# Self-attention: first pass on a three-bank ring, some key pairs as rectified differences

## The reference

```python
qkv = h @ w_qkv + b_qkv
q, k, v = jnp.split(qkv, 3, axis=-1)
q = q.reshape(B, S, H, DK)
k = k.reshape(B, S, H, DK)
v = v.reshape(B, S, H, DK)
scores = jnp.einsum('bqhd,bkhd->bhqk', q, k) / np.sqrt(DK)
attn = jax.nn.softmax(scores, axis=-1)
o = jnp.einsum('bhqk,bkhd->bqhd', attn, v).reshape(B, S, D)
x = x + o @ w_o + b_o
```

## Time and profile before

| what | value |
|---|---|
| median of 3 runs | 2763.42 us (2761.18 to 2769.22) |
| profiled execution's own time | 2774.48 us |
| span of the profile | 2772.7 us |
| TensorE (matmul) busy | 2119.2 us, 76% |
| VectorE busy | 1248.5 us, 45% |
| ScalarE busy | 828.2 us, 30% |
| projection of queries, keys and values | about 538 to 598 us of the span |
| attention steps | about 606 to 1098 us of the span |

### The profile page before, as it was taken

How to read it: one execution, slowest core, us unless ns; L and a number is a source line. 1 busy time by engine, 2 the same in 40 slices (tenths; PEclk the granted TensorE clock), 3 DMA queues, 4 the chain that set the end, 5 groups by cost and what they waited for, 6 DMA issues and landing times. The chain is left out here.

```text
span 2772.7 us, 39418 instructions
## 1 busy us (share of the span) xinstructions
PE 2119.2 (76%) x11925; PEld 1548.1 (56%) x11929; DVE 1248.5 (45%) x2841; ACT 828.2 (30%) x1718; POOL 443.2 (16%) x363
## 2 busy tenths in 40 slices
PE   6689979368899898255999634899998981993398
PEld 5477746122222222144999533788888871683297
DVE  6856621868777773342333343222222222673221
ACT  2404421113555556001333210233333330341021
POOL 0100000010000000033222103334524530000322
PEclk9899989677999999557999865999999996995699
DMA  3012110130101100712222253222222212007111
GB/s 129 1 43 74 46 33 4 37 102 13 36 24 32 28 25 7 244 50 75 33 33 33 53 194 107 54 43 48 58 39 47 48 31 57 1 1 274 55 30 27
DMA packets 128820, 157.19 MB, mean 57 GB/s; under 512 B 24266, under 2 KB 108499, under 8 KB 128693
## 3 DMA queue, kind: packets, MB, share of 16 engines
q1 hardware_dynamic: 100661, 123.14, 14.3%
q0 software_dynamic: 28032, 32.60, 6.7%
HBM read 110.32 MB, written 57.24 MB: 60 GB/s over the span
## 5 line engine op out<-in xcount | busy, mean ns | idle before, releaser
L1454 PE MATMUL banks<-m_rowsT,x_normT 128*128 128x128 f32 x4032 | 487.0, 280 | 46.1 <-DVE m_rowsT L1516 22.9
L1454 PEld LDWEIGHTS banks<-m_rowsT,x_normT 128*128 128x128 f32 x4032 | 473.3, 195 | 76.8 <-issue 65.2
L1464 PE MATMUL banks<-e_w,m_hT 128*128 x2016 | 456.7, 379 | 3.6 <-ACT m_y L1549 2.6
L1464 PEld LDWEIGHTS banks<-e_w,m_hT 128*128 128x128 f32 x2016 | 373.1, 190 | 50.8 <-issue 5.4
L1539 ACT ACTIVATE m_hT<-banks,m_bias 128x128 f32<-128x128 f32 x848 | 241.1, 370 | 402.5 <-PE banks L1454 384.5
L1839 DVE TENSOR_REDUCE sh_mhalf<-banks 128x1 f32<-128x512 f32 x512 | 318.9, 684 | 76.1 <-PE banks L1742 71.4
L1817 ACT ACTIVATE sh_pT<-banks 128x1024 f32<-128x1024 f32 x256 | 249.5, 1021 | 210.5 <-PE banks L1795 210.5
L1411 POOL DMA_INDIRECT scratch_acc<-m_y,m_ids x106 | 175.8, 1659 | 538.0 <-ACT m_y L1549 487.2
L1520 DVE COPY m_ids<-m_rows 128x1 int32<-128x1 int32 x126 | 19.4, 154 | 509.7 <-POOLq L1417 410.5
L1742 PE MATMUL banks<-sh_ks,sh_qs 96*128 96x512 bf16 x512 | 196.1, 416 | 53.8 <-DVE sh_mhalf L1839 33.4
L1501 DVE TENSOR_SCALAR x_normT<-e_w 128x2048 f32 x129 | 159.7, 1238 | 137.6 <-PEq L1470 81.9
(11 more groups left out here) (317 smaller groups left out, 2485.5 us busy)
## 6 DMA issues: line engine op xcount, KB each, us to landing
e_w<-L_W SPq DMA_DIRECT2D x32, 1024.0 KB, 12.2
m_rows<-scratch_rows SPq DMA_DIRECT2D x126, 132.5 KB, 2.1
e_w<-L1f_W SPq DMA_DIRECT2D x16, 1024.0 KB, 12.1
a_bt<-bias SPq DMA_DIRECT2D x16, 616.0 KB, 4.1
scratch_parts<-sp_part SPq DMA_DIRECT2D x48, 128.0 KB, 1.9
sh_qs<-scratch_parts SPq DMA_DIRECT2D x96, 64.0 KB, 2.6
sh_ks<-scratch_parts SPq DMA_DIRECT2D x96, 64.0 KB, 2.7
scratch_acc<-x_resid SPq DMA_DIRECT2D x2, 2048.0 KB
```

The lines of the kernel that those rows point to most:

```text
L1454: mm = pe.matmul(ps[:, H_BANK + f // 4, f % 4 * P:(f % 4 + 1) * P], w1_tile[:, u, k, f * P:(f + 1) * P], rowsT[:, u, k, :], start=(k == 0) ...
L1464: mm = pe.matmul(ps[:, Y_BANK, 0:D], hT[:, u, f, :], w2_sb[:, bass.ds(e, 1), f, :], start=(f == 0), stop=(f == FB - 1))
```

## The change

In the **projection** ScalarE writes the high part straight from the bank (`high`), VectorE the rest (`rest`), ScalarE the middle (`middle`), VectorE the low (`low`). The orders are written with one chunk of lead: high(n), then middle(n-1); rest(n), then low(n-1). For keys ScalarE also writes the full values (`keys`), and VectorE takes the difference of keys 0 to 511 and keys 512 to 1023 (`step`), which goes through the same split and to DRAM (`store_steps`).

In the **first pass** a pair can be *rising*: its first product is with the key differences (`kd`), ScalarE takes Relu of it, and VectorE adds the second product and takes the row maximum in one operation, since max(a, b) = b + relu(a - b). All pairs of steps 0 and 1 are rising, and pairs 1, 4, 7, 10 and 13 of each later step. The banks are a ring of three (0, 1, 7), shared with the two turns, and of seven in the opening; ahead of step 0 TensorE waits for all of the opening's maxima. The two halves' maxima are joined by one operation and turned once; the split into parts is made after the turn by four linked operations on 16x128. Loads of differences come on SyncE's queue (18 transfers a step instead of 12); the queries of step 0 come on ScalarE's.

```diff
+RISING_PAIRS = (1, 4, 7, 10, 13)
...
+            r32, k32, d32 = sb2("r32", [P, 2, CH]), sb2("k32", [P, 2, CH]), sb2("d32", [P, 2, CH])
...
+            part_d = [sb2(f"part_d{i}", [P, 2, CH], BF16) for i in range(PARTS)]
...
+
+                def store_steps(m):
+                    j, b = 2 + m // 2, m % 2
+                    sp.wait_ge(d_split, m + 1)
+                    for i in range(PARTS):
+                        sp.dma_start(parts_d[i, (j % 2) * P:(j % 2 + 1) * P, b * CH:(b + 1) * CH], part_d[i][:, m % 2, :]).then_inc(d_stored[m % 2], 16)
+
                 for n in range(NQ):
                     j, c = n // NCH, n % NCH
                     sp.wait_ge(split, n + 1)
                     for i in range(PARTS):
                         sp.dma_start(parts[j // 2, i, (j % 2) * P:(j % 2 + 1) * P, c * CH:(c + 1) * CH], part[i][:, n % 2, :]).then_inc(stored[n % 2], 16)
+                    if n >= K0 + 3 and n % 2:
+                        store_steps((n - K0 - 3) // 2)
+                store_steps(3)
...
                     if n >= 4:
-                        pe.wait_ge(q_sb, n - 3)
+                        pe.wait_ge(rest_done, n - 3)
+                    if n >= K0 + 4:
...
                 w.wait(act)
-                for n in range(NQ):
-                    j = n // NCH
+
+                def high(n):
+                    j, u = n // NCH, n % 2
                     act.wait_ge(mm_done, n + 1)
                     if n >= 2:
-                        act.wait_ge(split, n - 1)
-                    act.activation(q32[:, n % 2, :], ps[:, n % 4, :], ACT.Identity, bias=bqk[:, j:j + 1]).then_inc(q_sb, 1)
+                        act.wait_ge(stored[u], 48 * (n // 2))
+                    act.activation(part[0][:, u, :], ps[:, n % 4, :], ACT.Identity, bias=bqk[:, j:j + 1]).then_inc(high_done, 1)
+
+                def keys(n):
+                    if n >= K0 + 2:
+                        act.wait_ge(d_done, (n - K0) // 2)
+                    act.activation(k32[:, n % 2, :], ps[:, n % 4, :], ACT.Identity, bias=bqk[:, n // NCH:n // NCH + 1]).then_inc(k_sb, 1)
+
+                def middle(n):
+                    act.wait_ge(rest_done, n + 1)
+                    act.copy(part[1][:, n % 2, :], r32[:, n % 2, :]).then_inc(middle_done, 1)
+
+                def step_high(m):
+                    act.wait_ge(d_done, m + 1)
+                    if m >= 2:
+                        act.wait_ge(d_stored[m % 2], 48)
+                    act.copy(part_d[0][:, m % 2, :], d32[:, m % 2, :]).then_inc(d_high, 1)
+
+                def step_middle(m):
+                    act.wait_ge(d_rest, m + 1)
+                    act.copy(part_d[1][:, m % 2, :], d32[:, m % 2, :]).then_inc(d_middle, 1)
+
+                for n in range(NQ):
+                    high(n)
+                    if n >= K0:
+                        keys(n)
+                    if n:
+                        middle(n - 1)
+                    if n >= K0 + 2 and n % 2 == 0:
+                        step_high((n - K0 - 2) // 2)
+                    if n >= K0 + 3 and n % 2:
+                        step_middle((n - K0 - 3) // 2)
+                middle(NQ - 1)
+                step_high(3)
+                step_middle(3)
...
+
+                def rest(n):
+                    j, u = n // NCH, n % 2
+                    dve.wait_ge(high_done, n + 1)
+                    if n >= K0:
+                        dve.wait_ge(k_sb, n - K0 + 1)
+                    if n >= 2:
+                        dve.wait_ge(split, n - 1)
+                    dve.scalar_tensor_tensor(r32[:, u, :], ps[:, n % 4, :], bqk[:, j:j + 1], part[0][:, u, :],
+                                             ALU.add, ALU.subtract).then_inc(rest_done, 1)
+
+                def low(n):
                     u = n % 2
-                    dve.wait_ge(q_sb, n + 1)
+                    dve.wait_ge(middle_done, n + 1)
                     if n >= 2:
                         dve.wait_ge(stored[u], 48 * (n // 2))
-                    link(dve.tensor_copy(part[0][:, u, :], q32[:, u, :]))
-                    link(dve.tensor_tensor(r32[:, u, :], q32[:, u, :], part[0][:, u, :], ALU.subtract))
-                    link(dve.tensor_copy(part[1][:, u, :], r32[:, u, :]))
                     dve.tensor_tensor(part[2][:, u, :], r32[:, u, :], part[1][:, u, :], ALU.subtract).then_inc(split, 1)
+
+                def step(m):
+                    dve.wait_ge(k_sb, 2 * m + 2)
+                    if m >= 2:
+                        dve.wait_ge(d_split, m - 1)
+                    dve.tensor_tensor(d32[:, m % 2, :], k32[:, 0, :], k32[:, 1, :], ALU.subtract).then_inc(d_done, 1)
+
+                def step_rest(m):
+                    dve.wait_ge(d_high, m + 1)
+                    dve.tensor_tensor(d32[:, m % 2, :], d32[:, m % 2, :], part_d[0][:, m % 2, :], ALU.subtract).then_inc(d_rest, 1)
+
+                def step_low(m):
+                    dve.wait_ge(d_middle, m + 1)
+                    if m >= 2:
+                        dve.wait_ge(d_stored[m % 2], 48)
+                    dve.tensor_tensor(part_d[2][:, m % 2, :], d32[:, m % 2, :], part_d[1][:, m % 2, :], ALU.subtract).then_inc(d_split, 1)
+
                 w.wait(dve)
+                for n in range(NQ):
+                    rest(n)
+                    if n:
+                        low(n - 1)
+                    if n >= K0 + 3 and n % 2:
+                        step_low((n - K0 - 3) // 2)
+                    if n >= K0 + 2 and n % 2 == 0:
+                        step_rest((n - K0 - 2) // 2)
+                    if n > K0 and n % 2:
+                        step((n - K0) // 2)
+                low(NQ - 1)
+                step_rest(3)
+                step_low(3)
                 for t in range(NT):
                     dve.wait_ge(v_mm, t + 1)
                     dve.tensor_tensor(vh[:, t, :, 0:DK], ps[:, 4 + t % 4, 0:D].rearrange("p (h d) -> p h d", d=DK),
...
-            A_BANK, B_BANK, O_BANK, T_BANK = 0, 2, 6, 7
+            B_BANK, O_BANK = 2, 6
+            OPENING, STEADY = (0, 1, 7, 2, 3, 4, 5), (0, 1, 7)
...
+            RISING = tuple(RISING_PAIRS if s >= 2 else range(2 * KT) for s in range(NP))
...
+            opening = [("a", 0, c) for c in range(NA)] + [("a", 1, c) for c in range(4)] + [("m", 0, 0)] + [("a", 1, c) for c in range(4, NA)]
+            steady = []
+            for s in range(NP):
+                for k in range(KT):
+                    steady += [("a", s + 2, 4 * k + c) for c in range(4) if s + 2 < NP]
+                    steady += [("m", s + 1, 0)] if k == 1 and s + 1 < NP else []
+                    steady += [("o", s - 1, 0)] if k == 2 and s else []
+            steady.append(("o", NP - 1, 0))
+            bank, user_before, last_user = {}, {}, {}
+            for i, use in enumerate(opening + steady):
+                bank[use] = OPENING[i % len(OPENING)] if i < len(opening) else STEADY[(i - len(opening)) % len(STEADY)]
+                user_before[use] = last_user.get(bank[use])
+                last_user[bank[use]] = use
+
+            def bank_free(pe, use):
+
+                old = user_before[use]
+                if old is None:
+                    return
+                kind, s, c = old
+                if kind == "m":
+                    pe.wait_ge(mT_sb, s + 1)
+                elif kind == "o":
+                    pe.wait_ge(on_done, s + 1)
+                elif c % 2 == 0 and c // 2 in RISING[s]:
+                    pe.wait_ge(a_rise, rise_count[s * NA + c + 1])
+                else:
+                    pe.wait_ge(a_max, max_count[s * NA + c + 1])
...
+                    steps = lambda i: parts_d[i, hp * 2 * DK:(hp + 1) * 2 * DK, b * CH:(b + 1) * CH].rearrange("(h p) n -> p h n", p=DK)
                     for j, (i, k) in enumerate(PROD):
-                        sp.dma_start(qs[u][j * DK:(j + 1) * DK, :, :], rows(0, i)).then_inc(stack_in[u], 16)
+                        sp.dma_start(kd[u][j * DK:(j + 1) * DK, :, :], steps(k)).then_inc(stack_in[u], 16)
+                        if s:
+                            sp.dma_start(qs[u][j * DK:(j + 1) * DK, :, :], rows(0, i)).then_inc(stack_in[u], 16)
                         sp.dma_start(ks[u][j * DK:(j + 1) * DK, :, :], rows(1, k)).then_inc(stack_in[u], 16)
...
+                bank_free(pe, ("a", s, c))
+                keys = kd[u][:, h, :] if half == 0 and c // 2 in RISING[s] else ks[u][0:SR, h, half * CH:(half + 1) * CH]
+                pe.matmul(ps[:, bank["a", s, c], :], qs[u][0:SR, h, t * P:(t + 1) * P], keys, start=True, stop=True).then_inc(a_mm, 1)
...
@@ -1748,26 +1875,25 @@
...
+                    bank_free(pe, ("m", s, 0))
+                    pe.transpose(ps[0:2 * KT, bank["m", s, 0], 0:P], m32[:], core.ident[:]).then_inc(mT_mm, 1)
...
+                    bank_free(pe, ("o", s, 0))
...
+                for c in range(4):
...
+                pe.wait_ge(a_rise, rise_count[2 * NA])
+                pe.wait_ge(a_max, max_count[2 * NA])
...
```

(42 more changed lines are left out.)

79 lines of the change are left out of this document (34 added, 45 removed).

## The result

| | median | runs | ratio to before, 95% interval |
|---|---|---|---|
| before | 2763.49 us | 2761.18 to 2769.22 | |
| changed | 2698.31 us | 2697.05 to 2704.05 | 0.9765 [0.9745, 0.9786] |

The change takes 65.2 us off. The prediction was 2725, range 2702 to 2756: the direction is right, the size is not, and the time lies 3.7 us under the range. A second measurement of the same kernel (experiment 1) gave 2703.97, inside the range.

The account below looks back on a forecast made before the run. The prediction took a latency bound, bank ring, reduction, bank ring, with no engine full. Terms: opening -18.5, step 0 -6.2, steps 1 to 13 -53, last two -0.2, projection +40, sum -38 us: 2725 us, range 2702 to 2756.

Parts of the forecast that it names:

- The bank ring bounds the steady step: Steady attention steps: the two-bank ring costs 0.67 us a block; three banks make a block 2.92 us, 3.5 less over six.
- new wait of score product 3: Blocks k = 0, 1 of a step: score product 3 waits 0.7 us for exponential 1, queued behind pair 1's Relu.
- The projection serialises on stores: Projection: the look-ahead order with two buffers puts one full store round trip into each chunk, +40 us.
- Rival 2: Projection: it does not serialise, because an order was misread, and keeps its pace; 2685 us, chance 0.07.
- rival 3: Steady steps: each Relu brings two table loads, as Relu and Exp are in different sets; 2825 us, chance 0.04.
- Step 0: First attention step after the opening: 26 us instead of 32.16 with TensorE kept busy, 6.2 us less.
- SyncE's queue hidden: Loads of differences: 18 x 0.467 = 8.4 us per step against 24.6, and the opening's 48 transfers, cost no time.
- The sum-and-max: Custom VectorE operation of the rising pairs: 0.75 us, 0.80 per pair with a wait in it.
- Rival 1: Opening and steps: sum-and-max at half rate, 1.29 us pitch; 33 us more, 2758 us, chance 0.13.
- The opening: First passes ahead of step 0: 32 pairs on seven banks at 0.80 us each, 18.5 us less.
- The steady step: Steps 1 to 13 of attention: 24.6 us instead of 28.71, 4.1 less each, 53 us less together.
- the difference is taken from either: Whole program: the same -38 us applied to the median (2725 us) or to the profiled execution (2736 us).

Follow-up runs that it names:

- experiment 1: The kernel before and the changed kernel each measured again with no edit: 2759.06 us (one run) and 2703.97 us (ratio 0.9781).
- Experiment 6: Changed kernel's later steps: two banks without rising pairs 2772.09 us, with five 2773.64; three banks without 2717.69, with five 2703.97.
- norise: Changed kernel with no rising pairs from step 2 on, three-bank ring and opening kept: 2717.69 us, ratio 0.9822 to the kernel before.
- experiments 3 to 5: Changed kernel with four buffers for the parts (2663.51 us), with the older chunk first on two buffers (2676.55), and with both (2660.19).
- before: The kernel before the change, in its first measurement and profile: median 2763.49 us.
- null_before: The kernel before, measured and profiled once more with no edit: 2759.06 us (one run).
- projonly: The changed kernel's projection in front of the attention of the kernel before: 2795.17 us, ratio 1.0107 to the kernel before.
- after: The changed kernel in its first measurement and profile: 2698.31 us, ratio 0.9765 to the kernel before.
- after_again: The changed kernel measured and profiled once more with no edit: 2703.97 us, ratio 0.9781 to the kernel before.

## Why the prediction came out as it did

**Right.**
- *The bank ring bounds the steady step.* Experiment 6 shows it by itself: 28.90 to 24.71. Blocks were forecast at 2.92, and those of k = 3 to 6 are 2.82 to 2.95 (k = 2 with the turns is 3.42, before 3.99; k = 7 with the step's last weighted sums 3.77, before 4.37); in the pair of blocks k = 0, 1 the forecast was 5.46 with a new wait of score product 3 for the exponential behind the Relu. It is 5.36 (814.23 to 819.59), and the wait is there, 0.43 us instead of 0.7:

```profile
817.52 0.60 PE L1921 MATMUL banks<-sh_qs,sh_ks 99*128 99x512 bf16 x2 [0.43 <-ACT sh_pT L1962]
```

  Without rising pairs (`norise`) that pair of blocks takes 5.42: the wait behind the Relu stands where a wait for a bank would stand.

- *The projection serialises on stores.* The walk put high(2) 6.7 us after the first chunk (measured 543.10 - 536.41 = 6.69), query chunks at 5.02 (4.97), key chunks at 5.62 (5.70 on average), the values 38.3 us later plus 1.4 for trips longer than the usual one (measured 38.5 in all, and 1.1 more in the values themselves). The 1.4 was not well founded: seven trips with one of 4.5 us have a mean of 3.2, not 3.05, and the earlier trace rows show only two of the seven. In the new trace one key chunk of seven took 0.5 us more than the others. Rival 2 (2685, no serialising) is refuted by the 43.7 us of waits, and experiments 3 to 5 turn the mechanism off in two ways. The Trainium skill ("DMA: Bandwidth & Descriptors", Anatomy of one DMA) gives its figures for a transfer that GpSimd issues, and by them a transfer would be 2.3 us, an estimate. These stores are issued by SyncE, which the prediction passed over; the row after is 1.9 again, and the chain by the row was the better one.
- *Relu brings no table load in the steps* (rival 3, 2825). ScalarE loads a table once in the attention stage, at its first exponential:

```profile
664.80 1.21 ACT L1950 ACTIVATE sh_rise<-banks 128x512 f32<-128x512 f32 x2
666.03 1.28 ACT L1962 ACT_TABLE_LOAD   x1
```

  That agrees with the Trainium skill ("ScalarE: Activation LUTs", Table sets), which lists relu in every set.
- *Step 0* at -6.2 (-6.3), and SyncE's queue hidden. That the number of step 0 fits this well is luck: in the repeat it is -7.6, with the clock's change at another place.

**Mis-sized.**
- *The sum-and-max.* I took 0.75, and 0.80 with waits, from the nearest three-operand row, though the range's lower end, a reduction's pitch of 0.60, was the truth: 0.61. The row that was nearer in shape (a 512-element read from PSUM with an accumulated result) was the reduction itself. Rival 1 (half rate, 2758) is refuted: one operand in PSUM and one in SBUF, both fp32, run at the full pitch, as the Trainium skill's sentence taken at its word allowed ("Vector Engine (DVE) Microarchitecture Reference", Points that are easy to get wrong).
- *The opening*: TensorE's pace at the lower clock counted for six pairs only, the sum-and-max was shorter, and the sum had a slip of 0.2 (its terms give 634.6, not 634.8). Six distances between pairs were about 0.85, most of the later ones 0.61, so that from the first sum-and-max to the first score product 22.6 us passed, not 27.3; the first one came 1.3 later than forecast, since the keys' stack landed later than I had it. VectorE's last sum-and-max starts at 666.69, the join of the maxima at 667.41, and the first score product 0.06 later: the new wait ahead of step 0 decides as the prediction said. -22.0 instead of -18.5.
- *The steady step*: 24.15 instead of 24.6. The six blocks gave 3.65 us, where 3.5 less 0.2 for the turn was forecast: the turn's bank held by the maxima costs about 0.1 and not 0.2 (the product behind the turn starts 0.54 after its score product, elsewhere 0.44). The pair k = 0, 1 gave 0.91 instead of 0.8. 13 x 0.46 = 6 us.

**The step that failed** is the last line of the sum: "the difference is taken from either", that is, from the median or from the profiled execution. With the right terms the sum would have been -48 and the median 2715, inside the range. The other 17 us are what no term held: I put the rest of the program down as one fixed time, with 0 us for it in the sum and nothing for its spread in the range, though I had the sign that it isn't fixed: the profiled execution lay 11 us over the median. The terms of the opening (-18.5, measured -22.0) and of the steps (-53, measured -59.2) were too small besides. Taking each kernel's stretch from its median leaves the rest of the program:

| kernel | stretch | median | rest |
|---|---|---|---|
| before, four measurements | 556.2 | 2763.49, 2763.14, 2763.36, 2758.66 | 2207, 2207, 2207, 2202 |
| changed, twice | 508.3, 508.2 | 2698.31, 2703.97 | 2190, 2196 |
| new projection, old attention | 594.0 | 2795.17 | 2201 |
| no rising pairs; two banks; neither | 514.8; 573.9; 575.2 | 2717.69; 2773.64; 2772.09 | 2203; 2200; 2197 |
| five pairs in the opening | 518.2 | 2724.92 | 2207 |
| four buffers; older first; both | 460.9; 477.5; 464.1 | 2663.51; 2676.55; 2660.19 | 2203; 2199; 2196 |
| four buffers, eight pairs | 476.9 | 2676.14 | 2199 |

The rest is 2190 to 2207 us, with no order by how long the stretch is. The first measurement of the changed kernel has the shortest of all; its repeat was 59.4 under before, not 65. So about 48 us lie in the stages that the change touches. Of the other 11 to 17 the spread of the code around explains a part, but the kernel before lies at the upper end three times out of four.

A few us go with the change although they lie behind it. From the last copy of bank 6 to the first product of the routed feed-forward that follows, the three profiles with the old attention (`before`, `null_before`, `projonly`) took 184.6, 184.6 and 184.4 us, and the ten with the new one 178.9 to 183.5 (the changed kernel 179.7 and 182.2). The code there is the same. In the first 20 us of this part the mean granted clock is 0.83 in the three and 0.91 in nine of the ten; the tenth, two banks and no rising pairs, has 0.83 and the 183.5. So 2 to 5 us of the changed kernel's gain are likely an effect of the new attention on the clock behind it. No run isolates this, and how the rest divides stays open.

By the spread of the rest, 17 us from end to end, the range would have had to reach some 8 us further on either side for this alone.

**A version that beats both** is four buffers with the changed kernel's order, 2663.5 us (ratio 0.9645). With both remedies it is 2660.2 (0.9653), which the medians can't tell apart; by the stretch the buffers alone are 3 us better.

## What to carry to other kernels

When a write order looks one item ahead on an in-order queue, ask whether the older item's last steps stand behind a wait that only an earlier item's store can end; with two buffers that is one full store round trip an item, and two more buffers, or the older item first, take it away. Before you lighten an engine's work, look for the ring that its latency closes: the third bank gave 4.2 us a step, the rising pairs 0.02 without it and 0.56 with it, nearly all of that in the two blocks where the rising pair comes first, and eight in other places were 0.98 dearer than the five. And when one stage of a long program is changed, measure that stage between two landmarks of its own, and give the range the spread of all the rest.

## What the runs showed of the hardware that was not expected

- The custom sum-and-max of 128x512, one operand in PSUM and one in SBUF, both fp32, is 0.689 us long and starts every 0.61 us, like a plain maximum reduction (0.682 and 0.60). The read of its accumulator (0.08 us) lies under the next one.
- In the opening TensorE's granted clock went from 0.50 to 1.00 behind a stretch in which it was busy 5.98 of 5.98 us (`after`). Before, it stayed at 0.50 in the whole opening with PE busy 39.77 of 48.40 us.
- The same code got a granted clock of 1.00 in one execution and 0.88 in the next. At two such places the same instructions fell 5.2 and 5.8 us behind (`after_again` against `after`), while the stretch itself repeated within 0.3 us. Another 13 us between two profiles of the kernel before came at a clock of 1.00 in both, in a routed feed-forward.
- The same code behind the attention had a mean clock of 0.83 in its first 20 us after the old attention and of 0.91 after the new one in nine of ten profiles; up to the routed feed-forward's first product it took 184.4 to 184.6 us against 178.9 to 183.5.
